# ScalarE takes the last quarter of the one-hot rows of a top-8 expert layer

## What is computed

```python
q = jnp.einsum('bnd,de->bne', x, w_q)
q = (q - mean) * jax.lax.rsqrt(var + BN_EPS) * bn_gamma + bn_beta
sim = jnp.einsum('pbnhd,hkpd->pbnhk', q, keys)           # 8 heads, 32 keys in each half
sx, ix = jax.lax.top_k(sim[0], TOPK)                     # TOPK = 8
sy, iy = jax.lax.top_k(sim[1], TOPK)
scores, pk = jax.lax.top_k(all_scores, TOPK)             # of the 64 sums of a head
indices = jnp.take_along_axis(all_indices, pk, axis=-1)  # one of 1024 experts
h = gelu_new(jnp.einsum('bnd,bnhkd->bnhk', x, down_embed[indices]))
h = jax.nn.softmax(scores, axis=-1) * h
out = jnp.einsum('bnhk,bnhkd->bnd', h, up_embed[indices])
```

## Time and profile before

| | |
|---|---|
| median of three runs | 1341.62 us |
| the profiled execution | 1341.98 us |
| its span, first to last instruction | 1340.2 us |
| mean granted TensorE clock | 0.898 of full |
| TensorE busy | 1156.0 us, 86% |
| VectorE busy | 1152.7 us, 86% |
| ScalarE busy | 876.6 us, 65% |
| GpSimd busy | 620.2 us, 46% |

### The profile page before, as it was taken

How to read it: one execution, slowest core, us unless ns; L and a number is a source line. 1 busy time by engine, 2 the same in 40 slices (tenths; PEclk the granted TensorE clock), 3 DMA queues, 4 the chain that set the end, 5 groups by cost and what they waited for, 6 DMA issues and landing times. The chain is left out here.

```text
span 1340.2 us, 32623 instructions
## 1 busy us (share of the span) xinstructions
PE 1156.0 (86%) x12753; PEld 900.3 (67%) x12758; DVE 1152.7 (86%) x2860; ACT 876.6 (65%) x1202; POOL 620.2 (46%) x512
## 2 busy tenths in 40 slices
PE   3576999999999999999999999999995639777778
PEld 2463677777777767776777777777674628677668
DVE  5796899999999999999999999998884288999984
ACT  0246888889888888888888888888872632222121
POOL 2344667566675667757577575775220000000000
PEclk9768999999999999999999999999997766666666
DMA  7007999999999999999999999999997000000000
GB/s 156 1 6 139 191 191 187 203 200 190 200 192 201 193 194 196 199 198 198 193 200 198 195 199 193 184 184 173 189 193 162 11 0 2 5 5 6 5 5 6
DMA packets 671121, 185.78 MB, mean 139 GB/s; under 512 B 655828, under 2 KB 668536, under 8 KB 670840
## 3 DMA queue, kind: packets, MB, share of 16 engines
q1 hardware_dynamic: 670968, 183.71, 80.3%
HBM read 19.51 MB, written 0.82 MB: 15 GB/s over the span
## 5 line engine op out<-in xcount | busy, mean ns | idle before, releaser
L1046 PE MATMUL ps<-pT,xa_hi 128*128 128x128 f16 x2288 | 381.1, 217 | 17.5 <-DMA pT<-p 16.7
L851 ACT ACTIVATE e<-ps,bias 128x1444 f32<-128x1444 f32 (+1 forms) x208 | 305.7, 1470 | 132.6 <-DVE bias L923 132.0
L1042 PE MATMUL ps<-pT,xa_hi 128*128 128x128 f16 x2288 | 382.8, 217 | 8.5 <-ACT uT L874 8.2
L1043 PE MATMUL ps<-pT,xa_lo 128*128 128x128 f16 x2288 | 382.8, 217 | 0.0
L921 DVE TENSOR_REDUCE nmax<-ps 128x1 f32<-128x1444 f32 (+1 forms) x208 | 343.9, 1653 | 19.3 <-PE ps L1026 18.6
L933 DVE TENSOR_TENSOR p<-e,p 128x1408 f16<-128x1408 f32 (+3 forms) x288 | 303.9, 1096 | 35.6 <-ACT p L859 34.5
L859 ACT ACTIVATE p<-e 128x1408 f16<-128x1408 f32 (+1 forms) x208 | 288.2, 1386 | 13.3
L811 POOL TENSOR_TENSOR p<-e,p 128x1408 f16<-128x1408 f32 (+1 forms) x128 | 196.6, 1556 | 182.9 <-ACT p L859 182.9
L1042 PEld LDWEIGHTS ps<-pT,xa_hi 128*128 128x128 f16 x2288 | 222.1, 98 | 33.6 <-issue 19.1
L1046 PEld LDWEIGHTS ps<-pT,xa_hi 128*128 128x128 f16 x2288 | 222.0, 98 | 24.2 <-DMA pT<-p 24.0
L1024 PE MATMUL ps<-xT_hi,q_hi 128*128 128x512 f16 (+1 forms) x624 | 229.9, 368 | 8.0 <-DMA xT_lo<-xa_lo 7.4
(11 more groups left out here) (225 smaller groups left out, 1910.4 us busy)
## 6 DMA issues: line engine op xcount, KB each, us to landing
raw<-in_ctx SPq DMA_DIRECT2D x16, 704.0 KB
pT<-p SPq DMA_TRANSPOSE x416, 4.2
f_wq<-in_L_ffn_w_q SPq DMA_DIRECT2D x1, 1024.0 KB, 4.9
f_wqt<-in_ffn_wq_t SPq DMA_DIRECT2D x2, 512.0 KB, 7.0
raw<-in_ctx SPq DMA_DIRECT2D x48, 18.0 KB
x_tok<-in_x SPq DMA_DIRECT2D x1, 800.0 KB
out_x<-ost SPq DMA_DIRECT2D x6, 128.0 KB, 2.0
wk_t<-in_wk_t SPq DMA_DIRECT2D x1, 512.0 KB, 5.7
```

What stands on the lines that cost most here:

```text
L851: act.activation(e32[t % E_BUF][rows, :], score_banks(t)[rows, 0:T], ACT.Exp, bias=bias[rows, t % N_BUF:t % N_BUF + 1]).then_inc(e_done, 1)
L1042: pe.matmul(out, hi, ph, start=n == 0, stop=False)
L1043: pe.matmul(out, lo, ph, start=False, stop=False)
L1046: pe.matmul(out, hi, pl, start=False, stop=False)
```

## The change

Rows 96 to 127 of `oneh` are made by ScalarE in place of VectorE. For row e, ScalarE writes the absolute value of `rT` minus e (32 instructions, each over the step's tokens of a half; the minus e comes from a column of a new tile `minus_row`, which GpSimd fills once), waits for the last of them, and then one instruction over all 32 rows writes the larger of zero and one minus that value, in place. For whole numbers this is 1 where `rT` equals e, and 0 elsewhere. VectorE's comparison covers rows 0 to 95. `expert_rows` waits for both.

```diff
+E_DVE = 3 * P // 4
...
+        minus_row = sb("minus_row", [P, P - E_DVE])
...
             pool.tensor_copy(iota_f[:, :], iota_i[:, :]).then_inc(fc_done, 1)
+            pool.wait_ge(fc_done, 6)
+            pool.tensor_scalar(minus_row[:, :], iota_f[:, E_DVE:P], -1.0, None, ALU.mult).then_inc(minus_done, 1)
...
                 act.activation(w_hi[0:j, 0:w], ps[0:j, 4, 2 * P:2 * P + w], ACT.Copy).then_inc(selT_done, 1)
+                act.wait_ge(minus_done, 1)
+                act.wait_ge(selT_done, 3 * i + 1)
+                if i:
+                    act.wait_ge(g_ps, group_number(i, 0))
+                for e in range(E_DVE, P):
+                    ins = act.activation(oneh[0:j, e, 0:w], rT[0:j, 0:w], ACT.Abs, bias=minus_row[0:j, e - E_DVE:e - E_DVE + 1])
+                ins.then_inc(far_done, 1)
+                act.wait_ge(far_done, i + 1)
+                act.activation(oneh[0:j, E_DVE:P, 0:w], oneh[0:j, E_DVE:P, 0:w], ACT.Relu, bias=1.0, scale=-1.0).then_inc(oneh_act, 1)
...
-                dve.tensor_tensor(out=oneh[0:j, :, 0:w], in0=iota_w[0:j, :, 0:w],
-                                  in1=rT[0:j, 0:w].rearrange("p (a s) -> p a s", a=1).to_broadcast([j, P, w]), op=ALU.is_equal)
+                dve.tensor_tensor(out=oneh[0:j, 0:E_DVE, 0:w], in0=iota_w[0:j, 0:E_DVE, 0:w],
+                                  in1=rT[0:j, 0:w].rearrange("p (a s) -> p a s", a=1).to_broadcast([j, E_DVE, w]), op=ALU.is_equal)
...
                 if n == 0:
                     pe.wait_ge(oneh_done, i + 1)
+                    pe.wait_ge(oneh_act, i + 1)
```

More of the change, by code:

```diff
@@ L1142, in ffn @@
         wide_idx, soft_done = sem("wide_idx"), sem("soft_done")
+        minus_done, far_done, oneh_act = sem("fminus_done"), sem("ffar_done"), sem("foneh_act")
         block = ctx.enter_context(nc.Block())
```

## The result

The change makes the kernel slower: 1356.12 us median (1354.16 to 1357.73, four runs) against 1342.78 (1341.55 to 1344.81, four runs), a ratio of 1.0097 with an interval of 1.0075 to 1.012. Timed again with six runs of the change and thirteen of the kernel before, the ratio is 1.0085 (1.007 to 1.01), which is 11.4 us. The forecast was 11.3 us slower, 1352.9, in a range from 1346 to 1360; the first measurement is 13.3 us slower.

A forecast was written before the change was run, and what follows sets the result against it. TensorE's wait for VectorE's one-hot chain bounds the expert layer; ScalarE's longer chain replaces it. Six full steps of 1.26 us plus 3.7 in the last give 11.3 us slower, 1352.9 us, range 1346 to 1360.

The forecast's parts named there:

- What bounds: Expert layer: TensorE waits for VectorE's `mv_lo` before L1560; a shorter `oneh` pays one us for one if `mv_lo` stays last.
- VectorE's part: `oneh` on VectorE loses 4096 elements per partition at 0.522 ns: 2.14 us less in each full step.
- ScalarE's part: Full step: 32 Abs 0.295 us apart take 9.53, Relu 3.61; TensorE starts L1560 1.26 us later, 7.6 in six steps.
- The last step: Step with half the elements per row: ScalarE's chain ends late, TensorE starts 3.7 us later; VectorE's shorter part gains nothing.
- The sum: Six full steps of 1.26 us plus 3.7 in the last: 11.3 us slower, 1352.9 us on the median.
- The cover: Gelu queued behind ScalarE's Relu ends near 1188.0; TensorE's second `hidden` needs it at 1194.0, so six us are left.
- The clock: TensorE's granted clock around L1560 and the second stretch: a rise may shift between turns, at most 0.6 us a turn either way.
- The faster issue (0.25): ScalarE's Abs issue 0.25 us apart, as from PSUM: nothing in six steps, last 2.3 later; 1343.9 us, chance 0.08.
- The rival on the other side: VectorE stays last at L1560, Abs distance 0.16: its 2.14 us gained six times, 1328.8 us; chance 0.04 with all gains.
- No overlap: ScalarE's instructions writing one tile stand end to end, 12.4 us, 2.9 more a step: 1373.2 us; chance 0.03.
- the signs named for the changed profile: Expected trace readings, among them wait before groups put down to Relu, about 8.5 us, and VectorE waiting 3.4 longer for `rT`.

The follow-up runs named there:

- VectorE's part alone: Against the change: ScalarE makes its 32 rows in the first step only, later steps reuse them; ratio 0.993 to the kernel before, 1333.15 us.

## Why the prediction was right

- **What bounds.** The step that TensorE waits for VectorE, and that a shorter `oneh` pays in full, was right: with VectorE's part alone all 2.14 us come off each of the five steps in which ScalarE makes no rows.
- **VectorE's part.** 6.55 us were expected, 6.56 are measured.
- **ScalarE's part.** The distance taken from L264 was 0.295 and is 0.292; 32 Abs take 9.45 us where 9.53 were expected. The Relu takes 3.62 (3.61), so the 0.09 of a column for its constant doesn't show. The start was off by 0.1 us: the first Abs starts 0.16 us behind the start of `w_hi` and overlaps with it, as `w_hi` does with `cT`, and so starts 0.57 us behind the start of `rT` where 0.67 were put. With the 0.08 of the Abs, 0.02 less before the Relu and 0.04 more behind it that makes the 0.15 by which a step was forecast too long: 1.11 us more, not 1.26.
- **The last step.** 3.43 us where 3.7 were forecast, for the same reasons: the first Abs starts 0.42 behind `rT`, not 0.58, and the 32 take 7.73 and not 7.84. TensorE's idle time there is 3.08, where 3.7 was named: it is done with `add_experts` 10.19 - 3.08 = 7.11 us behind `rT`, and before it started the groups at 6.76.
- **The sum.** 11.3 forecast. The trace gives 10.1 for the terms, 10.2 and 9.7 for the whole layer in two profiles, and the timing 11.4 with 9.4 to 13.4 as its interval. The first measurement has 13.3, 3.2 us above the forecast's 1352.9, of which 1.2 is that the kernel before came out at 1342.78 and not at 1341.62. That the second came so close to the terms' sum is partly chance: the terms were 1.2 us too large, and how much of the rest is ahead of the layer can't be told at this resolution.
- **The cover.** The gelu behind the Relu ends at 1194.79, and TensorE reaches its second `hidden` some 8 us after 1192.55. No wait for it was added: the list has one of 1.7 us on `gel`, as before.
- **The clock.** TensorE was idle 7.96 to 8.64 us in the second to sixth turn, where it was 6.88 to 7.79, and the granted clock had fallen to the lower level, 0.50, before it started, as before. The window rows of the changed kernel in the pause of the third step, where the clock is the third number from the end:

```profile
1186.00:1188.00 2.00, 0.00 (x0) 0.00 (x0) 2.00 (x3) 2.00 (x8) 0.00 (x0) 0.86 0.00 0
1188.00:1190.00 2.00, 0.00 (x0) 0.00 (x0) 2.00 (x11) 1.97 (x4) 0.00 (x0) 0.50 0.00 0
```

  The second stretch is 25.20, 25.08, 25.50 and 25.25 us in the first four turns, where it was 25.56, 25.57, 24.98 and 25.61. Over all six turns its sum is 144.7 us, where it was 144.9. A single turn changed by 0.52 at most, which is within the 0.6 us that were allowed.
- **The rivals.** The faster issue (0.25) has its measured counterpart in the PSUM source, 0.250, and even then the kernel isn't faster. The rival on the other side needed a distance below 0.25; without the column the distance is 0.20, and the step does drop to 10.8 us, with ScalarE still last by 0.24 us, as the full gain was said to need a distance below 0.19. The mechanism was right, its condition isn't met with a column. No overlap is excluded: 9.45 us and not 12.4.

Two of the signs named for the changed profile were wrong, without harm to the cause. First, the wait before the groups was to be put down to the Relu. It was in one step out of seven, and to "issue" in the others. Second, VectorE was to wait 3.4 us a turn longer for `rT`. It waits 11.4 us there in seven times, as before (11.9). The prediction looked at the wrong wait: VectorE's spare time shows one wait earlier, at `weigh` (`wgt` in the list), which needs TensorE's groups. It is 33.8 us there, where the kernel before has 11.3. The 22.5 more are 3.2 a turn over seven turns, which is about the lead of VectorE's end over ScalarE's (3.19 in the third step). VectorE runs ahead until its next piece that depends on TensorE, and is level with it again from there.

## What to carry to other kernels

Before work is moved to an idle engine, price its whole chain there, from the common start to the common end, and compare it with the chain that it is to shorten; the idle share doesn't tell this. The best share is where both chains meet (here 25 rows of 128). Where a piece costs six times as much on the helper, a little beyond it is worse than a little short of it. A stage in which the old engine wasn't late gets nothing from the split, so the last, small step should be left alone.

## What the runs showed of the hardware

- The price of a small ScalarE instruction in a row depends on more than its elements. At 128 elements, written to SBUF, the starts are 0.200 us apart from SBUF without a column operand, 0.292 with one, and 0.250 with one from PSUM. At 64 elements it is (7.73 - 0.34) / 31 = 0.238 with a column from SBUF.
- From PSUM the duration of one grows along the row of 32, from 0.40 to 0.66 us, so the end of the last comes later than the distance between starts says.
- A second wait on a matmul costs nothing that shows: TensorE starts 0.05 to 0.06 us behind VectorE's `mv_lo`, with one wait (before) and with two (25 rows, no Relu). Where ScalarE comes last it starts 0.09 to 0.14 behind it, so the difference goes with the engine that comes last and not with the number of waits.
- Abs and Relu between the exp and the gelu brought no table load: there is one before the gelu, of 1.28 us, as before.
- The part up to the first `rT`, the same code but for the small GpSimd instruction, differs by up to 6 us between executions, for the most part in the cross-attention: the first `rT` stands between 1094.97 and 1100.93 in the eleven profiles. A difference of some 10 us in a late stage is read more surely from that stage of the trace than from the total.
